# Values' product with the probabilities as the loaded operand, in a transformer-like chain of two layers on one core

## The reference, cut to what matters

```
q = rmsnorm((x @ Wq).reshape(B, 512, 16, 128)); k, v likewise from ctx (v without the norm)
attn = softmax(q k^T / sqrt(128))            # over the 512 keys
out  = (attn @ v).reshape(B, 512, 2048) @ Wo # added to x
```

## Time and profile before

| | |
|---|---|
| median of three runs | 2015.83 us |
| the profiled execution | 2035.78 us, its span 2033.8 us |
| mean granted TensorE clock | 0.961 |
| PE matmul | 1876.3 us busy, 92% of the span |
| DVE | 1392.9 us, 68% |
| ACT | 1048.6 us, 52% |
| POOL | 310.4 us, 15% |

### The profile page before, as it was taken

One profiled execution on the slowest core, in us unless ns is written; L12 is line 12 of the kernel. 1 busy time (PEld: TensorE's weight loads), 2 busy tenths in 40 slices (PEclk: granted clock), 3 DMA queues, 4 the chain that ended last, 5 costly groups with the idle time before them and its releaser, 6 DMA issues.

```text
span 2033.8 us, 23853 instructions
## 1 busy us (share of the span) xinstructions
PE 1876.3 (92%) x7070; PEld 1073.2 (53%) x7103; DVE 1392.9 (68%) x1775; ACT 1048.6 (52%) x2256; POOL 310.4 (15%) x189
## 2 busy tenths in 40 slices
PE   6799889899999989999999899998899999998895
PEld 2455444556564455656544556564465656543442
DVE  3699726999997689999956999999254232344422
ACT  4667425755554466556536656563445444443430
POOL 1001210211111011212100212120022111114032
PEclk9799989999999989999999899998899999999997
DMA  5256221222222112222221222222224242302333
GB/s 164 80 165 198 83 88 33 68 83 85 85 82 98 39 47 78 85 84 84 79 73 43 73 78 90 75 93 73 78 99 93 64 90 62 88 30 100 125 108 124
DMA packets 115763, 176.23 MB, mean 87 GB/s; under 512 B 12512, under 2 KB 67552, under 8 KB 115184
## 3 DMA queue, kind: packets, MB, share of 16 engines
q1 hardware_dynamic: 101040, 158.58, 24.1%
q0 software_dynamic: 13840, 15.21, 3.7%
q10 hardware_dynamic: 816, 1.57, 0.2%
HBM read 146.76 MB, written 34.87 MB: 89 GB/s over the span
## 4 chain that ended last, share of the span: by engine, by line
PE 64%; issue 16%; DVE 11%; ACT 4%; POOL 2%; another core or an unknown queue 2%; DMA 1%; DVEq 0%; ACTq 0%; SPq 0%; POOLq 0%
PE ps L1881 21%; PE px L1881 14%; PE pp L1881 14%; PE pd L1881 6%; PE po L1881 5%; DVE arena L1396 3%; PE pp L2226 2%; DVE arena L1388 2%; ACT hbuf L1177 1%; ACT arena L913 1%; DVE arena L1407 1%; DVE arena L1414 1%; DVE arena L1374 0%; DVE arena L1372 0%
## 5 line engine op out<-in xcount | busy, mean ns | idle before, releaser
L1396 DVE TENSOR_TENSOR_SCAN arena<-arena 128x512 f32<-128x512 f32 x256 | 294.3, 1205 | 0.6
L762 POOL TENSOR_TENSOR rms<-ssv,minus_half 128x4 f32<-128x4 f32 x64 | 154.3, 2412 | 795.4 <-ACT ssv L1153 795.4
L1177 ACT ACTIVATE hbuf<-ps,shift,rms_k 128x512 f32<-128x512 f32 x256 | 198.5, 777 | 123.5 <-PE ps L1881 116.0
L1881 PE MATMUL ps<-qkT 128*128 128x512 f32 x512 | 256.0, 612 | 5.6 <-ACT hbuf L1177 3.0
L1881 PE MATMUL pp<-wq,xnT 128*128 128x256 f32 x1024 | 233.4, 382 | 2.9 <-issue 1.5
L1881 PEld LDWEIGHTS pp<-wq,xnT 128*128 128x128 f32 x1024 | 192.1, 190 | 40.7 <-issue 13.4
L1598 DVE SCALAR_TENSOR_TENSOR xc<-px,rden,xc 128x512 f32<-128x512 f32 x192 | 136.2, 740 | 85.0 <-PE px L1881 83.4
L1881 PE MATMUL px<-wo,oT 128*128 128x512 f32 x384 | 183.2, 599 | 0.4
L913 ACT ACTIVATE arena<-arena,a_neg 128x512 f32<-128x512 f32 x256 | 163.3, 710 | 14.4 <-DVE arena L1374 8.4
L1881 PEld LDWEIGHTS ps<-qkT 128*128 128x128 f32 x512 | 91.5, 194 | 132.2 <-ACT hbuf L1177 70.5
L1881 PE MATMUL pp<-ctx_att,wk 128*128 128x512 f32 x256 | 136.1, 676 | 22.5 <-ACT ssv_k L975 6.4
(11 more groups left out here) (324 smaller groups left out, 2901.7 us busy)
## 6 DMA issues: line engine op xcount, KB each, us to landing
bc<-bc_dram SPq DMA_DIRECT2D x56, 512.0 KB, 4.8
wo<-in_Wo SPq DMA_DIRECT2D x32, 512.0 KB, 3.6
wq<-in_Wq SPq DMA_DIRECT2D x32, 512.0 KB, 3.3
qkT<-kt_dram SPq DMA_DIRECT2D x32, 512.0 KB, 3.5
hbuf<-in_w SPq DMA_DIRECT2D x8, 1024.0 KB, 9.5
wk<-in_Wk SPq DMA_DIRECT2D x32, 256.0 KB, 2.8
wv<-in_Wv SPq DMA_DIRECT2D x32, 256.0 KB, 2.8
kt_dram<-xnT SPq DMA_DIRECT2D x14, 512.0 KB, 3.0
```

The source lines that it names most:

```text
L762: nc.gpsimd.tensor_tensor(rms[:, j], ssv[:, j], half, ALU.pow).then_inc(rms_done, 1)
L1177: nc.scalar.activation(pT[:, h, k], ps[s_use % 2][:], ACT.Exp, bias=shift[:, 0:1], scale=rms_k[:, bass.ds(G * (GH * NT) + (h * NT + k), 1) ...
L1396: V.tensor_tensor_scan(hb[i][:, e], dA[i][:, e], hb[i][:, e], 0.0, ALU.mult, ALU.add).then_inc(scan_done[i], 1)
L1881: return nc.tensor.matmul(out, lhsT, rhs, start=first, stop=last, **kw)
```

## The change

The two operands of the values' product change places: 128 queries' exponentials are now the loaded operand, and 129 columns stream, 128 values and a column of ones. So `values(h, k)` issues four products (eight passes) of 129 columns where it issued one product (two passes) of 512. The result is [query, value], with the denominator as the 129th column; three query tiles lie in the head's bank and the fourth in a `px` bank. `key_sums`, `denominators`, `denominators_out` and the tile `den` leave. `recip` now takes the reciprocal straight from PSUM in two instructions per head. ACT scales the rows (`o_scale`, four 128x128 copies per head), PE turns them back (`turned`, four transposes per head) into the head's bank, and ACT copies them to `oT` as before (`o_out`). As the rows are already divided, `out_proj` adds both heads' products in PSUM and `add_out` is one plain addition per token tile, four per group and not eight.

The places in the orders move as well. PE: `turned(g, 0)` ends the group, `turned(g-1, 1)` stands behind `q_rows(0)` of the next, `out_proj(g-1, 0)` and `(g-1, 1)` behind `v_rows(1)`, `out_proj(g-1, 3)` between `q_turned(0)` and `q_turned(1)`. ACT: a group begins with `o_out(G-1, 0)` and `o_scale(.., 1)`, `o_out(G-1, 1)` stands behind `mean_squares(0)`, and `o_scale(g, 0)` ends it. DVE: a group begins with `recip(g-1, 1)` and ends with `recip(g, 0)`, behind both `times_c` and both `add_y`. GpSimd sets the column of ones once per turn.

```diff
-        v_sb = sb("v_sb", [P, NT, GW])
+        v_ext = sb("v_ext", [P, NT, GH, D + 1])
+        v_sb, v_ones = v_ext[:, :, :, 0:D], v_ext[:, :, :, D]
...
+        o_rows = dsum[:].rearrange("p h (t d) -> p h t d", t=NT)
...
+                    def o_scale(G, g, h):
+                        act.wait_ge(rden_done, 2 * (G * GH + h) + 2)
+                        bank, _ = d_at(turn_, g, h)
+                        for k in range(NT - 1):
+                            nc.scalar.activation(o_rows[:, h, k], o_bank[h][:, k * (D + 1):k * (D + 1) + D], ACT.Copy,
+                                                 scale=rden[:, h, k:k + 1]).then_inc(o_scaled, 1)
+                        nc.scalar.activation(o_rows[:, h, NT - 1], px[bank][:, 0:D], ACT.Copy, scale=rden[:, h, NT - 1:NT]).then_inc(px_drained[bank], 1)
...
                     else:
+                        o_out(G - 1, 0)
+                        o_scale(G - 1, g - 1, 1)
                         decays(0)
                         squares(0)
                         mean_squares(0)
+                        o_out(G - 1, 1)
                         decays(1)
...
+                def add_out(g, k):
+                    if k < 2:
+                        bank, n = w_at(turn_, g, k)
+                        dve.wait_ge(px_full[bank], n)
+                        V.tensor_tensor(xc[:, k], xc[:, k], px[bank][:], ALU.add).then_inc(px_drained[bank], 1)
+                    else:
+                        dve.wait_ge(o2_full[k % 2], b * NG + g + 1)
+                        V.tensor_tensor(xc[:, k], xc[:, k], ps[k % 2][:], ALU.add).then_inc(o2_added[k % 2], 1)
...
                     if is_first(g):
                         if scan:
                             times_b(b + 1, g, 0)
                             scans(b + 1, g, 0)
                             gate_norm(b + 1, 3 * b + 3)
                             times_b(b + 1, g, 1)
+                            scans(b + 1, g, 1)
...
                     else:
+                        recip(g - 1, 1)
                         if scan:
                             times_b(b + 1, g, 0)
+                            times_b(b + 1, g, 1)
+                            scans(b + 1, g, 0)
+                            scans(b + 1, g, 1, range(0, 2))
+                        add_out(g - 1, 0)
+                        add_out(g - 1, 1)
                         if scan:
+                            scans(b + 1, g, 1, range(2, EC))
+                        add_out(g - 1, 2)
+                        add_out(g - 1, 3)
                     if scan:
+                        for i in range(GH):
+                            times_c(b + 1, g, i)
+                            add_y(b + 1, g, i)
+                    recip(g, 0)
                     if is_last(g):
+                        recip(g, 1)
                         if scan:
                             gate_y(b + 1)
+                        for k in range(NT):
+                            add_out(g, k)
...
+                        for j in range(NT):
+                            out = o_bank[h][:, j * (D + 1):(j + 1) * (D + 1)] if j < NT - 1 else px[bank][:, 0:D + 1]
+                            m = mm(out, pT[:, h, k, j * P:(j + 1) * P], v_ext[:, k, h], k == 0 and j in (0, NT - 1), k == NT - 1, skip_group_check=True)
...
                         q_rows(0)
-                        out_proj(g - 1, 0, 0)
+                        turned(g - 1, 1)
                         q_rows(1)
                         v_rows(0)
                         v_rows(1)
-                        out_proj(g - 1, 0, 1)
+                        out_proj(g - 1, 0)
+                        out_proj(g - 1, 1)
                         for j in range(2):
                             pe.wait_ge(v_out[j], G + 1)
-                        out_proj(g - 1, 2, 0)
+                        out_proj(g - 1, 2)
                         q_turned(0)
-                        out_proj(g - 1, 2, 1)
+                        out_proj(g - 1, 3)
```

More of the change, by code:

```diff
@@ L791, in turn @@
                     key_rms(U_FIRST, 0, first_columns(2, 3))
+                _, full, _, n = at(turn_of(b, off), ("F1", NT - 1), HG - 1)
+                pool.wait_ge(full, n)
+                nc.gpsimd.memset(v_ones, 1.0).then_inc(ones_set, 1)
                 rstd(2, 3 * b + 2)
@@ L834, in gather @@
                         ).then_inc(g_in[b] if b < B - 1 else g_last_in[k], 16)
[L836 to L838 removed]
+            pool.wait_ge(o_copied, B * NG * GH)
             nc.gpsimd.memset(zero, 0.0).then_inc(zero_set, 1)
@@ L1222, in group @@
                         d_times_u(b + 1)
-                    for h in range(GH):
-                        o_out(h)
-                        denominators_out(h)
+                    o_scale(G, g, 0)
+                    if is_last(g):
+                        o_out(G, 0)
+                        o_scale(G, g, 1)
+                        o_out(G, 1)
                 for_groups(act, group)
@@ new lines, in add_out, with recip @@
+                def add_out(g, k):
[6 more added lines that the diff above has]
+                        V.tensor_tensor(xc[:, k], xc[:, k], ps[k % 2][:], ALU.add).then_inc(o2_added[k % 2], 1)
+                def recip(g, h):
+                    bank, n = d_at(turn_, g, h)
+                    dve.wait_ge(o_full, (b * NG + g) * GH + h + 1)
+                    at = (NT - 1) * (D + 1)
+                    V.reciprocal(rden[:, h, 0:NT - 1], o_bank[h][:, 0:at].rearrange("p (t w) -> p t w", w=D + 1)[:, :, D]).then_inc(rden_done, 1)
+                    dve.wait_ge(px_full[bank], n)
+                    V.reciprocal(rden[:, h, NT - 1:NT], px[bank][:, D:D + 1]).then_inc(rden_done, 1)
@@ L1636, in group @@
                             layernorm(3, 2 + 3 * B, x3[2])
-                        key_sums(G, 0)
-                        if scan:
-                            scans(b + 1, g, 1)
                     else:
+                        recip(g - 1, 1)
                         if scan:
                             times_b(b + 1, g, 0)
-                        add_out(g - 1, 0, 0)
-                        if scan:
-                            times_b(b + 1, g, 1)
-                            scans(b + 1, g, 0, range(0, 2))
@@ L1647, in group @@
-                        add_out(g - 1, 0, 1)
-                        add_out(g - 1, 2, 0)
-                        if scan:
-                            scans(b + 1, g, 0, range(2, EC))
-                        add_out(g - 1, 2, 1)
-                        key_sums(G, 0)
-                        if scan:
-                            scans(b + 1, g, 1)
-                    key_sums(G, 1)
-                    if scan:
-                        times_c(b + 1, g, 0)
-                    recip(0)
-                    recip(1)
@@ L2294, in group @@
                         values(1, k)
-                        if k == 1:
-                            denominators(0)
-                    denominators(1)
+                    turned(g, 0)
                 for_groups(pe, group)
-                out_proj(NG - 1, 0, 0)
-                out_proj(NG - 1, 2, 0)
-                out_proj(NG - 1, 0, 1)
+                for k in range(NT):
+                    out_proj(NG - 1, k, range(1))
+                turned(NG - 1, 1)
+                for k in range(NT):
+                    out_proj(NG - 1, k, range(1, GH))
                 if scan:
```

137 lines of the change are left out of this document (47 added, 90 removed).

## The result

The changed kernel takes 2034.39 us, the median of four runs (2030.74 to 2037.16), where the kernel before takes 2015.6 on the same chip (four runs). The ratio is 1.0095, with an interval of 1.0064 to 1.0126: 18.8 us slower. The profiled execution took 2037.16 us, with a span of 2035.3.

What follows compares the result with a forecast made beforehand. PE's stream was taken to bound a group, with DVE nearly full beside it. Steady groups -9, first groups +26 and turn ends +3 gave +20, rounded to +22: 2038 us (+1.1%), range 2004 to 2070, with 0.50 on 2025 to 2055.

Steps and rivals of the forecast that it cites:

- The price of a pass: Values' product on PE: a two-pass float32 product of 129 columns hides its load and costs 0.110 us a pass.
- The rival in which a short pass pays for its load: Values' passes on PE: unhidden loads add 203 us over 32 groups, giving 2240, half-way 2140; chance 0.06.
- The steady group: 28 of 32 groups: head +0.7 us, the rest shorter, net -0.3 each, -9 in all; bounds 0 and -0.6.
- The stall: Before a steady group's scores: PE waits for the last output product's addition in a bank the scores need, 0.6 us.
- The first group: First group of three scanning turns: PE idles 7.2 us behind a late recip; 6.2 + 2.6 (slow clock) each, +26 us.
- The end of a turn: From the values' end to scan_a: o_out(1), gate and four additions start it later, +0.5 us, three times.
- fast rival: Whole kernel: PE's stream alone decides, with fast passes at turn ends; 1981 us, chance 0.09.
- The last turn: End of the last turn: the same chain as at other turn ends, with nothing beside it, costs about +2 us.
- The idle costs less: First and steady groups: no slow clock behind the idle, no stall at the scores; +5, so 2021 us, chance 0.20.
- The stream alone decides: Whole kernel: recip runs early enough, so PE's shorter stream gives 19 us and turn ends 16; 1981 us, chance 0.09.
- ACT becomes the bound in steady groups: At q_turned(0), margin 0.3 us: slower o_scale and a POOL slip of 1 us cost 28 us more; 2066, chance 0.15.
- DVE's relief worth nothing: DVE in each group: some 7 us less work on an engine that isn't the bound, worth nothing by itself.

Runs made afterwards that it cites:

- e2: Changed kernel with out_proj(g-1, 1), which lands in a px bank, last of the output products instead of out_proj(g-1, 3); ratio to before 0.9962, repeated 0.9978.
- e5: Changed kernel with eight unread float32 products of 512 columns put into PE's 7 us idle in the first group of scanning turns; ratio to before 1.0091.
- e3: Changed kernel with the edits of e1 and e2 together; ratio to before 0.9942, repeated 0.9938.
- e1: Changed kernel with both reciprocals moved ahead of the scan's additions in the first group of scanning turns; ratio to before 1.0039, repeated 1.0049.
- e6: e3 with the last two scans of a group moved behind the additions of products 2 and 3 on DVE; 1989.05 us, ratio to before 0.9877.
- e4: Kernel before with one of three key sums per head made, PE's stream unchanged; ratio to before 0.9997.
- e7: Changed kernel with a group's second times_b moved behind the first scan on DVE, to run beside POOL's power; run once, 2058.18 us.

## Why the prediction was right, and where not

The forecast of +1.1% (2038 us) met +0.95% (2034.39). The mechanism was right where the loss is, in the first groups and at the stall, and the sum came out partly because errors of opposite sign offset each other.

- **The price of a pass** (forecast 0.110, worked out from columns and the transposes' row): 0.111. The load hides. The rival in which a short pass pays for its load fell. The Trainium skill, "TensorE: Matmul & The Clock Gate", section "Back-to-back issue gap", would have put a pass near 0.16 by the prediction's estimate, and this trace doesn't agree.
- **The steady group** (forecast -0.3, 28 times, -9 us): -0.1 in the first three turns and +0.16 in the last (34.17 for 34.01), together about -1. The head was forecast at 19.15 and measured 19.24, the rest at 14.8 and measured 14.93. These are small errors, but the term is the difference between a gain of 1.0 and a loss of 0.7, so they took most of it. The stall was forecast at 0.6 and shows as 0.53 of idle; e2 priced it at 0.79 with the load that it uncovers.
- **The first group** (forecast 3 x (6.2 + 2.6) = +26): idle 7.12 where 7.2 was forecast, and `recip` behind `add_y(0)`, `times_c(1)` and `add_y(1)`, as written. The next group began 790.18 - 751.58 = 38.60 after the turn's first query product, for 31.10 before, so 7.5 later, and with the slow query products behind that start the cost in this turn is 8.5 us. The three turns together pay 24.7. Of the 7.5, 1.1 belong to a longer wait for the queries (4.98 for 3.86), which lies between 3.7 and 5.0 in the first three turns of either kernel. The clock's share was sized too large: 1.4 us, not 2.6, measured twice, in the rows and by e5. I had taken it from eight transposes and eight score passes behind another gap; here the last 3.9 us of the idle already were at the lower clock, and less of PE's work was left to be slow. The total is near; its split was not.
- **The end of a turn** (forecast +0.5, three times): wrong in sign and in number, since `scan_a` stands at the ends of only two turns. From the end of the values it starts at 15.56, where 15.9 stood before and 16.4 was forecast: the chain over `turned(1)`, the gate and the four additions is the one forecast, 0.8 shorter. Instead of one idle of 3.58 PE has three of 0.73, 0.73 and 1.27, and the eight passes last 3.51 from start to start for 5.12. That is -0.3 - 1.6, about -2 us, twice. At the third turn's end the key products behind the wait for DVE come 0.5 earlier, so the ends give about -4. The shorter idles alone don't make the passes fast: e3 has the same three, starts the passes at 15.56 as well, and they last 5.21. PE there in e3:

```profile
1027.39 5.37 PE L1864 MATMUL ps<-dsum,ipT 128*128 128x512 f32 x8 [1.27 <-DVE xc L1608]
1032.60 0.95 PE L1864 MATMUL pp<-ones,qk_raw 128*128 128x1 f32 x8
```

The passes are slow in both turns of both traces of e3, in both turns of e5 and in the first turn of e1, and fast in all other traces of the changed kernel and its versions. What decides it stays open, and with it whether the change can claim the 1.6. The prediction counted on fast passes there in its fast rival alone and left them out of its sum.

- **The last turn** (forecast +2): the last output product ends 10.07 us after the values for 8.31 before, +1.8. Its first group, for which nothing was forecast, is 1.1 shorter (29.11 for 30.25).
- **The sum.** With the last group of each turn counted to the end of its values, as the ends need it, the steady groups give about +0.4. Then 0.4 + 24.7 - 1.1 - 4 + 1.8 = +21.8, against the forecast of +20, a difference of 21.8 in the profiled spans without the idle, and a timed difference of 18.8. The steady groups were 8 to 9 us worse than forecast, and the ends of turns 5.5 us, the first groups 1.7 and the last turn's first group 1.1 better. That these nearly cancel is luck. Neither the forecast nor this sum has what happened elsewhere: the two stretches between the first three attentions gain another 2.6 us each behind `scan_a`, by a clock at 1.00 for 0.95, while the third one and the work ahead of the first attention lose 2.8 and 3.9.
- **The other rivals.** "The idle costs less" (2021) assumed no slow clock and no stall. Both are there, though the clock costs only 4 us in three turns. "The stream alone decides" (1981) is near what the changed kernel becomes when both causes are taken away: e6 gives 1989. "ACT becomes the bound in steady groups" fell; PE has no wait at `q_turned(0)`, and POOL's power, which stood in the chain with 3.11, takes 1.0 to 2.1.
- **DVE's relief worth nothing**: e4 shows it on the kernel before, for 83 of the 205 us. In the changed kernel it isn't DVE's load but the order of its queue that costs 16 us of attention time, of which 5 to 11 reach the timed ratios.

## What to carry over

When an engine's work is handed to another and something small is moved behind something large in a queue, follow the small instruction: 0.17 us of reciprocal behind 6.6 us of scan work cost three waits of 7 us, and shifting it forward moved part of the wait to the next reader of the same queue until that one was put in order too. Ask of each PSUM bank who needs it next: the last product before a phase should go to the bank that the phase doesn't need first, which here was worth 0.8 us in each of 28 groups. Where a gap was followed by slow passes, price them when a change opens or fills such a gap, but compare more than one trace first: behind the same three idles, the same eight passes took 3.5 us in one version and 5.2 in another. And follow an edit beyond the stage that it mends: e1 saved 16 us in the attention and gave up to 7 back between the attentions.

## What the runs showed of the hardware

- A power on POOL over 128x4 elements takes 1.01 to 1.04 us where DVE has nothing running as it starts. Where DVE has an instruction running, it ends 0.86 to 0.87 us after a 128x2048 product and 0.80 us after a 128x512 scan (48 powers before, 44 in after, 44 in e7; ten others start within 0.13 us of such an instruction's end or just ahead of one). So it takes 3.1 us (median of before) where a product of 2.3 us has just begun, 2.0 to 2.7 in e7 and 1.0 to 2.1 in after. Moving DVE's products shortened this step of the chain by 1 to 2 us, which nothing in the change aimed at.
- In an idle of 7.12 us on PE the granted clock fell to 0.50, and the next 5.74 us of work ran at 0.75, which cost 1.4 us; with PE kept busy in the gap (e5) it was 1.00. After idles of 0.73, 0.73 and 1.27 the clock stayed up in after, and eight passes took 3.51 us; after the same idles they took 5.21 in e3.
- A feed-forward stretch with the same passes of PE took 94.1 us at a granted clock of 1.00 in after, 96.7 at 0.96 in e1 and 98.4 at 0.95 in e3. Nothing here shows what decides it.
- In float32 a pass of 129 columns behind a load of 128 takes 0.111 us, no more than its columns.
- An idle of 20 us near the end comes and goes from chip to chip in both kernels. Nothing here shows what makes it.
